# A two-layer transformer with routed experts on one core: the numbers that lay out the order of all engines are exchanged

## The reference, cut to what matters

```python
x = L0_attn_x                                   # (16, 256, 128) float32
x = _layernorm(x + _L0_attn_ref(x, ...))        # 16 heads of 8, causal
x = _layernorm(x + _L0_ffn_ref(x, ...))         # 8 experts, best 2 of each token, 128 -> 256 -> 128, relu
x = _layernorm(x + _L1_attn_ref(x, ...))        # 16 heads of 8, not causal
x = _layernorm(x + _L1_ffn_ref(x, ...))         # 15 experts, best 3, gelu gate, and a shared expert
```

## Time and profile before

| | us |
|---|---|
| median of 3 runs | 1232.21 |
| lowest, highest | 1225.54, 1235.29 |
| the profiled execution | 1241.11 |
| its span, first to last instruction | 1239.3 |

### The profile page before, as it was taken

One profiled execution on the slowest core, in us unless ns is written; L12 is line 12 of the kernel. 1 busy time (PEld: TensorE's weight loads), 2 busy tenths in 40 slices (PEclk: granted clock), 3 DMA queues, 4 the chain that ended last, 5 costly groups with the idle time before them and its releaser, 6 DMA issues.

```text
span 1239.3 us, 22949 instructions
## 1 busy us (share of the span) xinstructions
PE 963.7 (78%) x7486; PEld 797.1 (64%) x7486; DVE 671.0 (54%) x2209; ACT 550.4 (44%) x1320; POOL 445.5 (36%) x695
## 2 busy tenths in 40 slices
PE   5899994968999778569998799686669827777840
PEld 4788883857999666457886576455448716656730
DVE  4476663644444557555556688654435603455643
ACT  1455652524655455346664577344356403222210
POOL 6010100254000644462005533554530370455565
PEclk9899997988999878889997899878879968888875
DMA  4666558343664233336853333322346935577312
GB/s 79 125 137 130 126 122 159 73 117 83 160 173 113 53 53 49 92 62 144 194 135 55 66 50 46 53 47 50 59 149 186 283 112 136 150 221 210 114 43 61
DMA packets 111510, 138.47 MB, mean 112 GB/s; under 512 B 12036, under 2 KB 85794, under 8 KB 111394
## 3 DMA queue, kind: packets, MB, share of 16 engines
q1 hardware_dynamic: 100002, 114.97, 41.2%
q0 software_dynamic: 10240, 20.99, 6.5%
q10 hardware_dynamic: 1152, 1.05, 0.5%
HBM read 70.25 MB, written 42.48 MB: 91 GB/s over the span
## 4 chain that ended last, share of the span: by engine, by line
PE 55%; another core or an unknown queue 14%; DMA 7%; issue 6%; DVE 6%; ACT 5%; SPq 4%; POOL 2%; ACTq 0%; DVEq 0%; POOLq 0%
PE bank_O L1112 7%; PE bank_N L1204 5%; PE bank_T L1090 5%; DMA QK<-parts 5%; PE bank_S L1063 4%; PE bank_FH L1192 4%; PE bank_S L1067 3%; ACT P L928 3%; PE bank_T L1094 3%; PE bank_S L1065 3%; PE bank_N L1120 2%; PE bank_T L1092 2%; PE bank_M L1036 2%; POOL G L871 2%
## 5 line engine op out<-in xcount | busy, mean ns | idle before, releaser
L1278 DVE TENSOR_REDUCE mp<-bank_S 128x3 f32<-128x384 f32 (+1 forms) x512 | 307.8, 619 | 211.0 <-PE bank_S L1067 95.9
L928 ACT ACTIVATE P<-bank_T 128x384 f32<-128x384 f32 (+1 forms) x512 | 259.3, 543 | 143.2 <-PE bank_T L1094 56.1
L871 POOL DMA_INDIRECT G<-yd,ypos x160 | 154.9, 968 | 136.2 <-issue 43.9
L855 POOL DMA_INDIRECT xs<-X,ypos x160 | 155.9, 975 | 51.4 <-issue 49.9
L1112 PE MATMUL bank_O<-P,V 128*32 128x256 f32 (+1 forms) x2048 | 137.8, 391 | 22.7 <-ACT OT L935 17.5
L1063 PE MATMUL bank_S<-QK 96*128 96x256 f32 x512 | 120.3, 334 | 18.5 <-DVE mp L1278 14.5
L1090 PE MATMUL bank_T<-QK 128*128 128x256 f32 x512 | 117.3, 334 | 16.9 <-ACT P L928 14.5
L1065 PE MATMUL bank_S<-rmat 128*128 128x256 f32 x256 | 92.6, 362 | 32.7 <-DMA QK<-parts 26.4
L1063 PEld LDWEIGHTS bank_S<-QK 96*128 96x128 f32 x512 | 85.7, 213 | 34.7 <-DVE mp L1278 24.7
L1090 PEld LDWEIGHTS bank_T<-QK 128*128 128x128 f32 x512 | 83.6, 211 | 35.3 <-ACT P L928 25.1
L1067 PE MATMUL bank_S<-QK 96*128 96x128 f32 (+1 forms) x512 | 104.8, 292 | 0.0
(11 more groups left out here) (170 smaller groups left out, 1797.7 us busy)
## 6 DMA issues: line engine op xcount, KB each, us to landing
QK<-parts SPq DMA_DIRECT2D x192, 128.0 KB
QK<-wtab SPq DMA_DIRECT2D x76, 257.0 KB
W<-w_in SPq DMA_DIRECT2D x46, 321.0 KB
QK<-xs SPq DMA_DIRECT2D x38, 256.0 KB
yd<-P SPq DMA_DIRECT2D x38, 256.0 KB
xs<-zeros SPq DMA_DIRECT2D x17, 512.0 KB, 7.7
xp<-xs SPq DMA_DIRECT2D x22, 256.0 KB
yd<-yb SPq DMA_DIRECT2D x22, 256.0 KB, 4.2
```

Of the source, the lines that this page charges most:

```text
L855: pool.indirect_dma_start(xs[g % 2], bass.IndirectOffsetOnAxis(ypos[L][:, 2 * b + blk, k:k + 1], 0), X[:, 2 * b + blk, :], None).then_inc( ...
L871: pool.indirect_dma_start(G[i][:, blk, k, :], None, yd[g], bass.IndirectOffsetOnAxis(ypos[L][:, 2 * b + blk, k:k + 1], 0))\
L928: act.activation(P[:, (h // 4) % 2, h % 4, 0:n], bank[("T0", "T1")[h % 2]][:, 0:n], ACT.Exp, scale=SCALE)\
L1278: dve.tensor_reduce(mp[:, a % 2, 0:n, h], bank[("S0", "S1")[h % 2]][:, 0:n * w] .rearrange("p (a c) -> p a c", a=n), AX.X, ALU.max).then_i ...
```

## The change

All numbers of PRM are exchanged, apart from a few that stay as they were. No step, duration in `plan()`, wait, tile or DMA is changed. The words with it: same steps, order of all engines laid out with scatters and gathers of a batch kept apart from one another. The diff is whole but for the 16 entries of "shift" that are used for no sequence (`starts` adds `shift[a]` from a = 16 on):

```diff
-PRM = {"l_stack": 5.73, "l_max": (8.41, 8.21), "l_x": (4.12, 6.22), "l_w": (8.18, 1.96), "l_y": (5.67, 3.93),
-       "period": (26.14, 21.28, 22.15), "first": (8.98, 7.51, 12.53, 12.66), "lag_s": (6.48, 8.09, 9.84, 7.91),
-       "step_s": (2.01, 2.14, 1.06, 1.16), "lag_t": (16.93, 17.18, 4.56, 3.79), "step_t": (0.0, 0.0, 3.12, 3.34),
-       "lag_o": (10.83, 13.03, 4.02, 3.03), "v": (106.33, 17.6, 400.0, 102.01), "lag_r": (12.81, 1.84, 0.0, 2.74),
-       "pre": (42.79, 162.17), "pre_w": (399.11, 305.04), "gap": 24.37, "f0": (7.1, 0.04), "f0_step": (2.77, 1.08),
-       "f0_g": (44.14, 72.2), "f0_gap": (389.83, 189.94), "f1": 34.47, "f1_step": (1.2, 7.65),
-       "f1_g": (69.92, 46.49), "f1_gap": (23.22, 1.59), "sh": (216.34, 400.0), "sh_step": (315.54, 184.61),
-       "scat": (141.84, 127.95), "xT": 174.08, "norm": (41.71, 3.29), "qk": (3.99, 360.99, 3.84),
-       "max": (3.8, 0.0, 180.76), "wv": (8.89, 9.13), "pj": (2.35, 1.3, 4.17, 2.73),
-       "rt": (6.29, 11.71, 23.0, 9.27, 26.11, 0.99, 23.9), "pg": (15.14, 6.89, 2.33, 8.12),
-       "wait": (0.03, 0.02, 0.23, 1.22, 0.21), "pe": 1.06, "qk1": (8.91, 240.89, 3.43), "max1": (1.19, 1.18, 6.72),
-       "wv1": (9.52, 2.94), "pj1": (0.0, 0.0, 1.45, 2.92), "rt1": (24.93, 9.21, 13.46, 10.31, 27.42, 3.33, 59.24),
...
-       "ld": (223.33, 397.68, 71.13, 177.31, 390.13), "clear": (136.8, 281.36)}
+PRM = {"l_stack": 5.74, "l_max": (8.36, 8.22), "l_x": (3.32, 3.36), "l_w": (7.85, 3.95), "l_y": (6.18, 6.97),
+       "period": (26.63, 21.53, 23.7), "first": (7.52, 9.35, 13.9, 11.63), "lag_s": (2.1, 14.12, 9.21, 7.47),
+       "step_s": (2.45, 2.0, 0.97, 1.12), "lag_t": (17.91, 18.5, 5.04, 4.25), "step_t": (0.0, 0.06, 3.55, 3.1),
+       "lag_o": (1.02, 15.48, 4.09, 4.38), "v": (129.88, 21.64, 203.32, 284.03), "lag_r": (16.2, 2.58, 0.0, 9.85),
+       "pre": (10.96, 198.39), "pre_w": (320.61, 293.78), "gap": 113.1, "f0": (0.83, 75.25), "f0_step": (1.98, 1.68),
+       "f0_g": (58.92, 4.77), "f0_gap": (397.47, 251.04), "f1": 9.1, "f1_step": (2.49, 7.79),
+       "f1_g": (321.08, 41.61), "f1_gap": (116.82, 134.18), "sh": (390.39, 184.86), "sh_step": (383.6, 400.0),
+       "scat": (181.01, 117.67), "xT": 295.67, "norm": (318.91, 0.0), "qk": (6.23, 251.78, 10.02),
+       "max": (5.39, 0.0, 71.03), "wv": (11.29, 9.12), "pj": (0.0, 0.0, 5.4, 1.85),
+       "rt": (2.72, 87.17, 26.52, 59.25, 29.42, 25.1, 24.97), "pg": (37.19, 21.51, 5.93, 7.01),
+       "wait": (0.04, 0.02, 0.24, 0.95, 0.1), "pe": 1.06, "qk1": (4.82, 261.05, 7.9), "max1": (3.01, 0.0, 4.91),
+       "wv1": (20.33, 1.54), "pj1": (0.3, 0.28, 4.38, 4.45),
+       "rt1": (38.99, 12.89, 96.18, 15.83, 56.04, 4.43, 224.49),
...
+       "ld": (28.25, 34.75, 20.69, 140.28, 69.0), "clear": (208.5, 220.61)}
```

More of the change, by code:

```diff
@@ L145, in shared_y_bank @@
     return ("N", "T1")[b % 2]
-PRM = {"l_stack": 5.73, "l_max": (8.41, 8.21), "l_x": (4.12, 6.22), "l_w": (8.18, 1.96), "l_y": (5.67, 3.93),
-       "period": (26.14, 21.28, 22.15), "first": (8.98, 7.51, 12.53, 12.66), "lag_s": (6.48, 8.09, 9.84, 7.91),
-       "step_s": (2.01, 2.14, 1.06, 1.16), "lag_t": (16.93, 17.18, 4.56, 3.79), "step_t": (0.0, 0.0, 3.12, 3.34),
-       "lag_o": (10.83, 13.03, 4.02, 3.03), "v": (106.33, 17.6, 400.0, 102.01), "lag_r": (12.81, 1.84, 0.0, 2.74),
-       "pre": (42.79, 162.17), "pre_w": (399.11, 305.04), "gap": 24.37, "f0": (7.1, 0.04), "f0_step": (2.77, 1.08),
[7 rows of a table removed]
-       "shift": (-7.0, -12.12, -22.3, -4.49, 9.46, 38.76, -3.48, 14.78, 43.78, -9.57, -11.79, -21.18, -36.13, 20.56, -52.02, -40.61, 0.81, -1.12, -3.49, -3.89, -1.08, -0.79, -1.48, -1.02, -0.82, 2.91, 0.79, 2.6, -0.85, 4.04, 3.6, 2.32),
-       "ld": (223.33, 397.68, 71.13, 177.31, 390.13), "clear": (136.8, 281.36)}
+PRM = {"l_stack": 5.74, "l_max": (8.36, 8.22), "l_x": (3.32, 3.36), "l_w": (7.85, 3.95), "l_y": (6.18, 6.97),
[3 more added lines that the diff above has]
+       "pre": (10.96, 198.39), "pre_w": (320.61, 293.78), "gap": 113.1, "f0": (0.83, 75.25), "f0_step": (1.98, 1.68),
[8 rows of a table added]
+       "shift": (60.0, -29.97, -44.53, -0.48, 40.32, 41.13, -36.87, -28.94, 60.0, 0.56, -9.8, -3.18, 0.51, 21.92, -6.72, 57.3, 3.95, -1.38, -0.93, -3.13, -0.41, 1.51, -1.64, 2.46, 1.05, 1.59, 4.33, 2.47, 0.59, 3.22, 2.08, 1.51),
+       "ld": (28.25, 34.75, 20.69, 140.28, 69.0), "clear": (208.5, 220.61)}
 def plan():
```

## The result

The changed kernel takes 1280.62 us (median of 5 runs, 1268.12 to 1283.82), the kernel before 1231.17 us beside it. The ratio is 1.0399, with a 95% interval from 1.0358 to 1.0441: slower by 4%, and above the range of the prediction (1185 to 1258 us), which had forecast 1212 us. The profiled execution of the changed kernel took 1268.12 us, that of the kernel before 1241.11 us.

The account below looks back on a forecast made before the run. Runs of POOL's indirect DMAs were taken to halt all engines. -23 + 3 = -20 us against the profiled 1241.1 gave 1221, by the factor 0.9928 1212 us; likeliest case 1187 to 1219, whole range 1185 to 1258.

Parts of the forecast that it names:

- What bounds the kernel: Whole kernel: no engine is full; a run of POOL's indirect DMAs halts all engines, and its length matters.
- Scatters and gathers apart, -23 us: POOL's queue: keeping touching batches apart wins 17.7 us plus half of 10.6, together 23 us; bounds 0 and 28.3.
- the runs stay: Rival on POOL's queue: the planner still issues the next scatter at once, or runs don't hold engines; 1225 to 1243, chance 0.25.
- The rest of the order, costed at nothing: All engines' orders laid out anew: no step added or removed, so work removed and added are both nothing.
- What is put between the batches, 0 with 9 kept: POOL, group 3's scatters: steps put between could wait for statistics; 9 us would show, charged 0, 9 kept for the range.
- The tail, +3 us: POOL's last gathers, group 3: three or four rstd move in front of the fourth gather, 3 us more.
- SP's queue, 0: SP: build_w1's due time falls from 390.13 to 69.00, but it is expected at the same place: 0.
- Slower, because group 2's combines pile up behind group 3's pages: Rival after attention: put-off combines stop POOL, each leftover batch costing 7.6 us at the end; 1245 to 1262, chance 0.33.
- The rule about who interferes: Skill's rule, set against the gain: POOL's DMAs could not hold ACT and PE, so keeping batches apart would give 0.

Follow-up runs that it names:

- the test: Kernel before, order untouched, with five chained fills (2.9 us) on POOL ahead of each of eight scatter batches directly following another: 1202.61 us, ratio 0.9795.
- the third row of part 1: Order of the kernel before up to the last weigh_V of sequence 31 (end of all attention), then the changed order; session without halts: 1068.92 us, ratio 1.0009.
- 147.6 us of fills: Kernel before with one 512-column fill on POOL between every two indirect DMAs, layer 1's gathers and tail included; session without halts: 1153.76 us, ratio 1.0839.

## Why the prediction was wrong, point by point

**What bounds the kernel.** Right: halts of all engines while POOL issues indirect DMAs. They are worth about 165 us of 1231 (1231 - 1066), with the lower clock behind them, more than the 73.9 + 6.7 + 26.1 us of PE's idle time in the scatters' stretches of the earlier trace rows, and a page of one execution can't tell that they might be absent on another day. The semaphore records behind the earlier trace rows show what a halt is: seven increments of PE's semaphores are recorded together from 902.95 to 903.20 us, 2 us behind POOL's run, and PE's last matmul before them ended by 894.2 us. PE had done its work, and the increments that tell of it came 9 us late.

**Scatters and gathers apart, -23 us. This is the step that failed.** Its price came out right as a sum, and that was partly luck: breaking up touching batches gives 27.7 us, against a bound of 28.3 worked out from the earlier trace rows, but about 5 us of it in the runs within attention (17.7 in the prediction) and 22.8 in the run of five batches (10.6). The prediction also priced every batch that followed another within 3 us, eleven of them, and the test broke up the eight with no step of POOL's in between. The step's premise was wrong: the step took the change to do what its name says. The diff gave the due times: a scatter of index i came 256 or 384 after the one before it, and now comes 235 or 353. The prediction wrote this down itself, as the rival "the runs stay", and gave it 0.25. And no case let the runs grow, though new numbers can move a run either way; 28 of the 50 us are there. With the 28 us added instead of taken off, the sum would have been 1241.1 + 28 + 3 = 1272, by the factor 1263.

**The rest of the order, costed at nothing. This failed too.** "No step is added or removed" was taken to mean that nothing but scatters, the tail and build_w1 mattered. The new order alone costs 19 us, and in the old order 7.7 us are lost by the later place of sequence 2's qk and its two copies. The rows to see it in were there: PE is busy for 49.4 of 50 us with nothing to spare, and a wait for a late stack was priced by the earlier trace rows at what it lasts. What the prediction had was a sum for named edits only; an order that is laid out anew has no unnamed part that is free. It could not have been read off single numbers of the diff. qk_lo's due time moved from 3.84 to 10.02, past the stack's (8.98 to 7.52), but `plan()` with the old numbers and the new "qk" alone leaves qk(2) where it was, right behind scores(1,5); the new "wait" alone, 0.04 for 0.03 on PE, moves it ten steps back, and the new numbers with the old "wait" put it back again. Laying out both orders and comparing them needs no chip and shows it, as it shows POOL's runs. (The line of "shift", which the diff leaves out whole, changed too in the 16 entries that layer 1 uses, by up to 3.5 us.)

**What is put between the batches, 0 with 9 kept.** Not tested by the change, since nothing was put between them. In the changed kernel POOL's wait for the statistics fell from 245.6 to 217.0 us. The fills show the other side: 2.9 us of other work at each of eight places gained, with halts.

**The tail, +3 us.** The size was near, the way was not. From the end of the last gather DMA to the end of the span it is 17.4 us after and 15.2 before. But no rstd moved in front of the fourth gather: all 36 gathers of the last run go in a row, and the last seven rstd come behind them (six in the row shown).

```profile
1202.86 1.01 POOL L872 DMA_INDIRECT G<-yd,ypos  x1 [0.84 <-DMA yd<-P]
...
1247.99 0.94 POOL L872 DMA_INDIRECT G<-yd,ypos  x1 [0.30 <-issue]
1248.96 4.01 POOL L802 TENSOR_TENSOR rstd<-rstd,half 128x2 f32<-128x2 f32 x6
```

**SP's queue, 0.** Right in the number, wrong in the reading of the due times. 390.13 does not lie before the due time of stack(8, 1), which is near 234, and 69.00 does not lie behind that of stack(3), which is 87. It comes to the same, because build_w1 has to follow stack(8, 1): in both orders it stands there, behind clear_xs(14). It goes out 12.7 us later than in the earlier trace rows and holds SP a little longer (14.65 for 13.93 us); the stop of PE, DVE and ACT behind it was 15.8 us and is 15.3 us.

```profile
191.19 6.59 SPq L705 DMA_DIRECT2D wtab<-xG  x1
197.82 8.06 SPq L706 DMA_DIRECT2D wtab<-b  x1
```

**The rivals.** Slower, because group 2's combines pile up behind group 3's pages: the sign was right by accident, the mechanism wrong. Six batches are left to gather when the last page is kept, before and after, POOL's wait for the combines is 32.7 us against 33.0, and the third row of part 1 puts the new order of that part at +0.09%. The runs stay: nearest to what happened, and still on the wrong side, since they grew. The case on the other side of it, runs that grow, was missing.

**The rule about who interferes.** The Trainium skill (SBUF — State Buffer, Who interferes with whom) says that only DVE and GpSimd share a port and that PE and ACT contend with nobody. In the sessions without halts the traces agree (PE busy for 40.2 of 40.5 us beside 30 scatters). In those with halts they don't (11.38 of 40.65), so the prediction was right to go by its own rows there.

## What to carry to other kernels

Check first that a change does what its name says: list the order of the engine in question before and after, from the numbers in the diff if need be, before a price is put on it. A list of due times that is searched anew has no part that stays as it was; where an engine is full, the place of each step that feeds a transfer is worth its wait and the lower clock behind it (here 5.3 us of wait, and then 0.65 for 8 us). And where a kernel issues runs of indirect DMAs, measure it in more than one session before you tune for it: gaps of 1.1 us after every second DMA took 6.1% off in one, and gaps of 0.5 us after every DMA cost 8% in another.

## What the runs showed of the hardware

- PE, DVE and ACT can halt together during a run of POOL's indirect DMAs, DVE's row maxima for up to 9.8 us in the kernel before, and the same program has no such halt in other sessions: 1230 to 1244 us against 1065 to 1066. Where POOL issues none, profiles of the two kinds of session keep step to some tenths of a microsecond. What differs between the sessions is open. The records name the chip by the same number for a session of either kind, so it need not be another chip.
- With halts, plain DMAs on POOL's queue in the same places did not cause them, at 557 ns each instead of 968 ns. A gap of 1.1 us between batches did as much by the time as one of 2.9 us (0.9820 and 0.9795), and gaps after every second DMA took off 6.1%. Whether a gap of 0.1 us would do is open: the kernel with such gaps ran only without halts, where they cost nothing (1.0015), and it would be the one to try first, since it could win in one kind of session and lose in none.
- Where nothing halts, 147.6 us of fills cost 89 us, on an engine that is busy for 42% of the span without them (446 us of 1074 in a profile without halts).
- The order behind the end of attention costs nothing with halts either, though its parts move. In the three profiles with the new order there and no fills, the first page of group 3 is kept 10 to 16 us sooner after the end of attention than in the kernel before, the pages take 15 to 21 us longer, and the tail 5 us less; from the end of attention to the end it is 304.6 to 305.5 us against 304.8. Without halts the third row of part 1 says the same (1.0009).
